# Cross rows of the ridge solves kept with the head innermost, and the complements' sides stored together

## The reference

```python
G = Kc.T @ Kc + RIDGE_EPS * I
W = jnp.linalg.solve(G, Kc.T @ Vc)
U = U0
for _ in range(POWER_K):
    U, _ = jnp.linalg.qr(W @ U)
Wr = U @ (U.T @ W)
S_new = DECAY_ALPHA * S + Wr
out = SCALE * (Qc @ S_new)
...
x = x + _L0_attn_ref(_layernorm(x, axis=-1), ...)
x = x + _L0_ffn_ref(_layernorm(x, axis=-1), ...)
```

## Time and profile before

| | |
|---|---|
| median of 3 runs | 900.69 us (897.38 to 904.1) |
| profiled execution, its own time | 900.93 us |
| its span in the profile | 899.1 us |
| mean granted TensorE clock | 0.958 |
| busy: TensorE, VectorE, ScalarE, GpSimd | 783.1, 631.7, 490.1, 227.4 us |
| TensorE weight loads, beside the matmuls | 530.6 us |
| DMA engines' mean busy share of queue 1 (SyncE's) and queue 0 (GpSimd's) | 36.8% and 7.5% |
| chain that ended last, by engine | TensorE 66%, VectorE 13%, issue 9%, DMA 5%, ScalarE 4% |

### The profile page before, as it was taken

The page is one execution under the profiler, slowest core; times in us unless marked ns, Lnnn a source line. Parts: engine busy times, 40 slices in busy tenths (PEclk is TensorE's granted clock), DMA queues, the critical chain, the costliest instruction groups (busy, mean ns, idle before and its releaser), DMA issues.

```text
span 899.1 us, 34359 instructions
## 1 busy us (share of the span) xinstructions
PE 783.1 (87%) x14730; PEld 530.6 (59%) x14730; DVE 631.7 (70%) x1336; ACT 490.1 (55%) x1068; POOL 227.4 (25%) x297
## 2 busy tenths in 40 slices
PE   4999999999999998988687687888798888899996
PEld 2555555565555555656455565666576666677775
DVE  3666399089998999980798988889953304666664
ACT  1864444555455454554444465556566665466665
POOL 4666100201001100000201012652012203555554
PEclk9999999999999999999879888999999999899999
DMA  8555211653455636655734645344456432222210
GB/s 313 155 159 167 77 62 42 205 177 122 139 162 160 185 72 168 185 162 168 162 79 119 188 116 159 103 135 116 107 154 138 104 93 69 62 82 74 77 43 30
DMA packets 174662, 114.43 MB, mean 127 GB/s; under 512 B 134128, under 2 KB 152944, under 8 KB 173488
## 3 DMA queue, kind: packets, MB, share of 16 engines
q1 hardware_dynamic: 168784, 91.00, 36.8%
q0 software_dynamic: 5728, 21.24, 7.5%
HBM read 61.22 MB, written 50.99 MB: 125 GB/s over the span
## 4 chain that ended last, share of the span: by engine, by line
PE 66%; DVE 13%; issue 9%; DMA 5%; ACT 4%; SPq 1%; POOL 1%; POOLq 0%; DVEq 0%; ACTq 0%
PE psum L1286 25%; PE psum L1332 6%; PE psum L1531 6%; PE psum L1541 5%; DVE outer L1142 4%; PE psum L1473 3%; PE psum L1511 3%; DVE work L1148 3%; PE psum L1504 2%; PE psum L1388 2%; PE psum L1375 2%; PE psum L1362 2%; PE psum L1423 2%; DVE state L1204 2%; PE psum L1497 1%
## 5 line engine op out<-in xcount | busy, mean ns | idle before, releaser
L1286 PE MATMUL psum<-wkv,xhat 128*128 128x512 f32 x512 | 240.3, 613 | 4.3 <-ACT xhat L834 4.3
L1142 DVE SCALAR_TENSOR_TENSOR outer<-work,rd 128x992 f32<-128x992 f32 (+30 forms) x248 | 189.6, 764 | 8.9 <-DVE rd L1136 0.3
L1148 DVE TENSOR_TENSOR work<-work,outer 128x992 f32<-128x992 f32 (+30 forms) x248 | 176.3, 711 | 8.6
L1286 PEld LDWEIGHTS psum<-wkv,xhat 128*128 128x128 f32 x512 | 93.2, 192 | 105.3 <-issue 99.5
L871 ACT COPY kv<-psum 128x512 f32<-128x512 f32 x128 | 75.1, 587 | 120.8 <-PE psum L1286 120.5
L1002 ACT ACTIVATE late<-psum,b1c,alpha 128x128 f32<-128x128 f32 x256 | 96.7, 461 | 49.6 <-PE psum L1531 49.6
L759 POOL TENSOR_TENSOR hsplit<-late,hsplit 128x512 f16<-128x512 f32 x64 | 77.4, 1211 | 142.4 <-ACT hsplit L1007 142.3
L1531 PEld LDWEIGHTS psum<-y3t,s1t 128*128 128x128 f16 x1024 | 61.3, 102 | 17.7 <-issue 16.7
L1531 PE MATMUL psum<-y3t,s1t 128*128 128x128 f16 x1024 | 66.9, 227 | 4.4 <-DVE y3t L1232 4.0
L1541 PE MATMUL psum<-s2t,hsplit 128*128 128x256 f16 x512 | 63.7, 279 | 4.0 <-POOL hsplit L759 2.7
L1332 PE MATMUL psum<-kv 128*64 128x128 f32 x1024 | 64.4, 280 | 0.0
(11 more groups left out here) (130 smaller groups left out, 1279.5 us busy)
## 6 DMA issues: line engine op xcount, KB each, us to landing
gc_d<-gc SPq DMA_DIRECT2D x32, 384.0 KB, 2.5
schur_mem<-gc_d SPq DMA_DIRECT2D x32, 384.0 KB, 4.2
f_d<-late SPq DMA_DIRECT2D x16, 512.0 KB, 3.6
late<-f_d SPq DMA_DIRECT2D x32, 256.0 KB, 2.7
sv_d<-sv SPq DMA_DIRECT2D x16, 384.0 KB, 3.1
lead_d<-work POOLq DMA_DIRECT2D x4, 1024.0 KB, 5.0
schur_mem<-lead_d SPq DMA_DIRECT2D x32, 128.0 KB, 4.3
r_d<-pt SPq DMA_DIRECT2D x16, 256.0 KB, 2.2
```

The lines of the kernel that those rows point to most:

```text
L1142: V.scalar_tensor_tensor(out=tile, in0=a[:, t, t + 1:HALF].unsqueeze(2).broadcast_to([P, m, HALF]), scalar=rd[:, t:t + 1], in1=a[:, t, t + ...
L1148: V.tensor_tensor(rest, rest, tile, ALU.subtract).then_inc(swept, 1)
L1286: ins = mm(dst[:], xnt[:, c, t], wkv[:, n, t, BANK * half:BANK * (half + 1)], start=t == 0, stop=t == KT - 1)
```

## The change

`pt`, `r_d` and `rr` are stored with the 32 columns outer and the 8 pairs of heads innermost. Per partition the load of `rr` is then one piece of 1 KB (32 x 8 numbers). The matmuls of SP and SX write PSUM, and those of SX and W read `pt` and `rr`, with a step of 8 numbers (32 bytes) from one column to the next. ScalarE's write of `lt`, whose layout stays, now steps by 128 bytes. `sv` and `sv_d` hold the 128 numbers of all complements first, then the 256 of all sides, so `vv` is loaded in pieces of 1 KB; ScalarE fills `sv` with two copies (128 x 256 and 128 x 512) in place of one. The unit matrices in `rr` are placed by four instructions in place of two. In the planner, MB of batch 2 or 3 is not put on the list before NB 7 or NB 15.

```diff
-                if t <= now["pe"]:
+                if t <= now["pe"] and (b < 2 or ("NB", CPB * (b - 1) - 1) in where):
                     del mask_at[b]
                     order.append(("MB", b))
...
-    r_d = scratch("r_d", [NCH, P, PAIRS, HALF])
-    sv_d = scratch("sv_d", [NCH, P, PAIRS // 2, 3 * HALF])
+    r_d = scratch("r_d", [NCH, P, HALF, PAIRS])
+
+    sv_d = scratch("sv_d", [NCH, P, PAIRS // 2 * 3 * HALF])
...
-        pt = sb("pt", [P, 2, 2, PAIRS, HALF])
+        pt = sb("pt", [P, 2, 2, HALF, PAIRS])
...
-        sv = sb("sv", [P, 2, PAIRS // 2, 3 * HALF])
+        sv = sb("sv", [P, 2, PAIRS // 2 * 3 * HALF])
...
-        rr = sb("rr", [P, 2, PAIRS, HD])
+
+        rr = sb("rr", [P, 2, HD, PAIRS])
...
-                    sp.dma_start(vv[:, i], sv_d[c + i][:, :, HALF:]).then_inc(solve_loaded, 16)
+                    sp.dma_start(vv[:, i], sv_d[c + i][:, P:].rearrange("p (s n) -> p s n", n=HD)).then_inc(solve_loaded, 16)
...
-                    sp.dma_start(rr[:, i, :, 0:HALF], r_d[c + i]).then_inc(sides_loaded, 16)
+                    sp.dma_start(rr[:, i, 0:HALF], r_d[c + i]).then_inc(sides_loaded, 16)
...
-                        src = sv_d[CPB * b:CPB * (b + 1), :, s, 0:HALF].rearrange("c (q i) n -> (c q) i n", q=QUADS)
+                        src = sv_d[CPB * b:CPB * (b + 1), :, HALF * s:HALF * (s + 1)].rearrange("c (q i) n -> (c q) i n", q=QUADS)
...
-                    nc.scalar.copy(rr[sl, :, :, HALF:].rearrange("p a h n -> p (a h) n"), eye).then_inc(eyes_placed, 1)
+                    for i in range(2):
+                        nc.scalar.copy(rr[sl, i, HALF:], ident[sl, sl].unsqueeze(2).broadcast_to([HALF, HALF, PAIRS])
+                                       ).then_inc(eyes_placed, 1)
...
-                    nc.scalar.mul(lt[rows(2 * a)].rearrange("p c h n -> p (c h n)"), src[rows(2 * a)], -1.0)
+                    nc.scalar.mul(lt[rows(2 * a)].rearrange("p c h n -> p c n h"),
+                                  src[rows(2 * a)].rearrange("p (c n h) -> p c n h", c=2, h=PAIRS), -1.0)
...
-                nc.scalar.copy(sv[:].rearrange("p c s n -> p c (s n)"), pieces(place("SV", e), BANK)[:, :, 0:12 * HALF]
-                               ).then_inc(drain("SV", e), 1)
+                src = pieces(place("SV", e), BANK)[:, :, 0:12 * HALF].rearrange("p c (s n) -> p c s n", n=3 * HALF)
+                nc.scalar.copy(sv[:, :, 0:P].rearrange("p c (s n) -> p c s n", n=HALF), src[:, :, :, 0:HALF])
+                nc.scalar.copy(sv[:, :, P:].rearrange("p c (s n) -> p c s n", n=HD), src[:, :, :, HALF:]).then_inc(drain("SV", e), 1)
...
-                dst = begin("SP", e)
+                dst = begin("SP", e).rearrange("p (c n h) -> p c n h", c=2, h=PAIRS)
...
-                            ins = mm(dst[sl, at:at + HALF], lp[sl, c, h, HALF:], lp[sl, c, h, 0:HALF], start=True, stop=True)
+                            ins = mm(dst[sl, c, :, h], lp[sl, c, h, HALF:], lp[sl, c, h, 0:HALF], start=True, stop=True)
...
-                                p, b = pt[sl, e % 2, c, h], gct[sl, e % 2, c, h, 0:HALF]
-                                ins = mm(dst[rows(2 * a + turned), at:at + HALF], b if turned else p, p if turned else b,
+                                p, b = pt[sl, e % 2, c, :, h], gct[sl, e % 2, c, h, 0:HALF]
+                                ins = mm(dst[rows(2 * a + turned), c, :, h], b if turned else p, p if turned else b,
...
-                                r, u = rr[side(a), c % 2, 2 * q + n], cu[side(a), n, c % 2, q]
+                                r, u = rr[side(a), c % 2, :, 2 * q + n], cu[side(a), n, c % 2, q]
```

More of the change, by code:

```diff
@@ L374, in build @@
         w2n = schur_mem[:, FT * DM:FT * DM + KT * FF].rearrange("p (t h) -> p t h", h=FF)
-        pt = sb("pt", [P, 2, 2, PAIRS, HALF])
-        xg = pt[:].rearrange("p e c h n -> p (e c h n)").rearrange("p (a k d) -> p a k d", a=2, k=2)
+        pt = sb("pt", [P, 2, 2, HALF, PAIRS])
+        xg = pt[:].rearrange("p e c n h -> p (e c n h)").rearrange("p (a k d) -> p a k d", a=2, k=2)
         lt = sb("lt", [P, 2, PAIRS, HALF])
-        sv = sb("sv", [P, 2, PAIRS // 2, 3 * HALF])
+        sv = sb("sv", [P, 2, PAIRS // 2 * 3 * HALF])
         lps = sb("lps", [P, 2, PAIRS // 2, HD])
         vv = sb("vv", [P, 2, PAIRS // 2, HD])
-        rr = sb("rr", [P, 2, PAIRS, HD])
+        rr = sb("rr", [P, 2, HD, PAIRS])
         cu = sb("cu", [P, 2, 2, PAIRS // 2, HD])
@@ L562, in load_solve @@
                 if e == 0:
-                    sp.wait_ge(eyes_placed, 4)
+                    sp.wait_ge(eyes_placed, 6)
                 if e % HALF_BATCH == 0:
@@ L618, in _ @@
                     sp.wait_ge(*is_drained("SX", c))
-                    sp.dma_start(r_d[2 * c:2 * c + 2].rearrange("c p h n -> p c h n"), pt[:, c % 2]
+                    sp.dma_start(r_d[2 * c:2 * c + 2].rearrange("c p n h -> p c n h"), pt[:, c % 2]
                                  ).then_inc(r_stored[c % 2], 16)
@@ L622, in _ @@
                     sp.wait_ge(*is_drained("SV", c))
-                    sp.dma_start(sv_d[2 * c:2 * c + 2].rearrange("c p s n -> p c s n"), sv[:]).then_inc(sv_stored, 16)
+                    sp.dma_start(sv_d[2 * c:2 * c + 2].rearrange("c p n -> p c n"), sv[:]).then_inc(sv_stored, 16)
                 elif step == "LS":
@@ L894, in leading_inverse @@
                 wait(act, r_stored[e % 2], 16 * (e // 2))
-                nc.scalar.copy(pt[:, e % 2].rearrange("p c h n -> p (c h n)"), place("SP", e)).then_inc(drain("SP", e), 1)
+                nc.scalar.copy(pt[:, e % 2].rearrange("p c n h -> p (c n h)"), place("SP", e)).then_inc(drain("SP", e), 1)
             def crosses(e):
@@ L902, in crosses @@
                 for a in range(2):
-                    nc.scalar.mul(lt[rows(2 * a)].rearrange("p c h n -> p (c h n)"), src[rows(2 * a)], -1.0)
+                    nc.scalar.mul(lt[rows(2 * a)].rearrange("p c h n -> p c n h"),
+                                  src[rows(2 * a)].rearrange("p (c n h) -> p c n h", c=2, h=PAIRS), -1.0)
                 for a in range(2):
-                    ins = nc.scalar.mul(pt[rows(2 * a + 1), e % 2].rearrange("p c h n -> p (c h n)"), src[rows(2 * a + 1)], -1.0)
+                    ins = nc.scalar.mul(pt[rows(2 * a + 1), e % 2].rearrange("p c n h -> p (c n h)"), src[rows(2 * a + 1)], -1.0)
                 ins.then_inc(drain("SX", e), 1)
@@ L1358, in leading_inverse @@
                     for h in range(PAIRS):
-                        at = HALF * (PAIRS * c + h)
                         for a in range(2):
                             sl = rows(2 * a)
-                            ins = mm(dst[sl, at:at + HALF], lp[sl, c, h, HALF:], lp[sl, c, h, 0:HALF], start=True, stop=True)
+                            ins = mm(dst[sl, c, :, h], lp[sl, c, h, HALF:], lp[sl, c, h, 0:HALF], start=True, stop=True)
                 ins.then_inc(fill("SP", e), 1)
             def crosses(e):
-                dst = begin("SX", e)
+                dst = begin("SX", e).rearrange("p (c n h) -> p c n h", c=2, h=PAIRS)
                 pe.wait_ge(*is_drained("SP", e))
@@ L1380, in complements @@
                 if e == 0:
-                    pe.wait_ge(eyes_placed, 4)
+                    pe.wait_ge(eyes_placed, 6)
                 dst = begin("SV", e)
```

## The result

The changed kernel takes 914.39 us (median of 4 runs, 912.71 to 919.84), the kernel before 899.04 (4 runs, 893.63 to 904.1): 1.018 of before, 95% interval 1.011 to 1.026. It is slower, by 1.1 to 2.6%. The profiled execution took 914.26 us, its span is 912.3.

What follows compares the result with a forecast made beforehand. TensorE was taken to bound 300 to 420 and 670 to 757 us, VectorE mostly 425 to 661. Costs of 9.4 us against gains of 7.0 gave +2.4 on 900.9, so 903.3 us, range 888 to 923.

Steps and rivals of the forecast that it cites:

- my likeliest case: Whole kernel: stepped operands cost part of a slowdown, offset by gains from fewer pieces; 896 to 911 us, chance 0.40.
- the halved pace: Rival: stepped operands halve TensorE's pace in W and SX, weight loads included; +20.1 us, 921 us, chance 0.27.
- The loss above 1%: Outcome for the whole kernel: slower than 910 us, beyond what a measurement can tell from no change; chance 0.32.
- Step of W: W reading `rr` with a step: 0.33 us more each, 14 of 32 counted, 4.6 us, ends 0 and 15.3.
- Step of SX: SX moving or loading stepped columns: 0.33 us more each, 12 of 16 counted, 4.0 us, top end 11.0.
- PSUM: Stepped PSUM writes of SP and SX: taken as 0, top end 13.6 us if SP takes twice as long.
- `lt`: ScalarE's stepped write between SX and SV: 588 ns to 0.92 us, mostly covered by a projection; 0.5 us, ends 0 and 8.
- `sv` in two copies: ScalarE's two copies for one: 0.17 us x 16, of which 0.3 us counts; 2.7 us without cover.
- The broken steps: TensorE gaps without instructions near `rr` and `cu` issues, 11.1 us: half the pieces, so -5.5 us, ends 0 and -11.1.
- The wait for `vv` at 669.54 us: Chain wait of 3.94 us after the last sweep: faster landing and issue give -1.5 us, ends 0 and -2.
- The queue of `cu`: SyncE's four issues of `cu`, 5.48 us, held up by what was already sent: expected well below 5.5 us.
- The planner's edit: Condition on MB of batch 2 or 3 after NB 7 or 15: always holds already, same list, worth 0.

Runs made afterwards that it cites:

- The kernel with 133,703 packets and no step: Kernel before with sides stored together and unit matrices kept in `pt` and `r_d`, so `rr` loads in 2-KB pieces, every operand contiguous; 902.69 us, 1.010 of before.

## Why the prediction was right or wrong

The forecast was 903.3 us with a range of 888 to 923; measured were 914.4, in the upper half, between my likeliest case (896 to 911) and the halved pace (921). The loss above 1% had a chance of 0.32. So the direction and the wide range held, and my own case did not: the halved pace is the rival whose mechanism the runs bear out, and my price for the step was less than half of the measured one.

- **Step of W.** I took 0.33 us more for each and gave the top end of twice as long. The chain shows 1.82 against 1.09, +0.73. For 14 steps that is 10.2 us, not 4.6. This is the first term that was mis-sized: I had priced TensorE's step by VectorE's 0.65 ns per number, and I had given the half that is loaded as weights no cost. Stepped weight loads went from 140 to 199 ns, and matmuls with a stepped moving operand from 224 to 288 ns in flight. SV with a stepped `lt` shows that a stepped load alone costs little beside a contiguous moving operand; how W's 0.73 us divide between its two halves no run shows.
- **Step of SX.** +0.33 taken, +0.94 measured (2.18 against 1.24), the top end. For 12 steps 11.3 us, not 4.0. The same error.
- **PSUM.** SP kept 1.13 us and 193 ns per matmul, so the 0 was right, and the end of 13.6 us was not needed.
- **`lt`.** 0.5 us taken, "a projection between these steps mostly"; 6.3 us more of waiting in SV. The projection is there, as I had it, and the timeline at 178 us shows why it doesn't cover: it and the transposes last 2.2 us, ScalarE's four instructions 3.3. Before, these took 2.4 us and were nearly covered, so almost all of the added 0.94 us shows. The duration went over my estimate, too (1058 ns, I had 0.92 us).
- **`sv` in two copies** (373 + 594 instead of 800 ns) and the units: nothing measurable, as forecast.
- **The broken steps.** I took half of 11.1 us. From 300 to 420 us all rows of "issue" fell from 8.1 to 0.5 us, from 670 to 770 from 7.0 to 5.9, 8.7 together. The sign and the order are right, by luck: the reason that I gave, half the pieces, is not borne out. The kernel with 133,703 packets and no step kept its stalls, and the one with all the packets and SX stepped lost a third of them. It looks as if part of what the step costs is taken out of time in which TensorE had nothing to issue.
- **The wait for `vv` at 669.54 us** is gone from the chain, as I had it, but nothing was gained by it: the last sweep's store starts 10.5 us later (672.50 against 661.97), and the next S starts at 685.17 us, 12.7 us after that store, where before it was 11.5.
- **The queue of `cu`**: 1.9 to 2.5 us for its four issues before 420 us where before the change it took 2.5 to 5.5, yet one of 3.6 us is left at 701.25 us, and the U step beside it is broken for 2.14 us.
- **The planner's edit**: the list is the same, worth 0.

The sum with the measured terms up to the fourth leading sweep: W 6 x 0.73 = 4.4, SX 11.3, `lt` 6.3, less 14.5 - 3.3 = 11.2 of stalls: +10.8. The chain shows 432.03 - 425.21 = +6.8. The 4 us between stay open; TensorE's clock, 0.97 in 300 to 420 us before and 1.00 after, could be 3.6 of them (an estimate, 3% of 120 us). It isn't the step that gave the clock: the kernel with the sides alone, where nothing steps, has 1.00 in that stretch as well.

That kernel is also the nearer neighbour for a sum, since the cross rows are all that parts it from the changed one. Its load starts at 413.7 us, so from there the rows cost 18.3 us. Its stalls from 165 us to the load are 8.1 us against 3.9, its SV waits 1.8 us for ScalarE against 8.0, and the terms give 4.4 + 11.3 + 6.2 - 4.2 = 17.7. So the prices of W, SX and `lt` account for this stage. The profile of the kernel before has 16.2 us of stalls in this stage, twice its neighbour's 8.1, so part of the fall in stalls that I read from it is the spread of single executions.

Of the 13.2 us between the spans of before and after, 6.8 are there at that load, 3.7 more come by the store of the last sweep, and 2.7 behind it. The eight W steps behind it would be 5.8 us alone; that part I didn't take apart.

The windows of the kernel after (stretch, PE, PEld, DVE, ACT, POOL busy with counts, clock, DMA share, GB/s), against the earlier trace rows:

```profile
300.00:420.00 120.00, 117.35 (x2520) 74.59 (x2514) 102.28 (x190) 68.20 (x132) 6.48 (x10) 1.00 0.55 161
...
670.00:760.00 90.00, 82.00 (x2272) 62.34 (x2271) 23.37 (x66) 54.53 (x134) 19.16 (x27) 1.00 0.41 117
```

TensorE is busy for 117.35 of 120 us, and still the stage ends 6.8 us later: the higher busy share here is more time for the same work.

## What to carry to other kernels

- Before an fp32 operand of TensorE is given a step for the sake of a DMA, look where two neighbouring columns lie: 8 bytes apart cost nothing here, 16 or 32 bytes apart took steps from 1.09 to 1.8 us and from 1.24 to 2.2, while a step whose weights alone were 32 bytes apart lost only 0.03. Heads in groups of two keep TensorE's pace and halve the pieces of `rr` (256 bytes instead of 128), though that gained no time here. And ScalarE did the reordering of `lt` for free (588 ns) by reading PSUM with a step and writing SBUF without one.
- Work that covers a wait covers it only up to its own length. Here 2.2 us of TensorE's work between two steps nearly hid ScalarE's 2.4 us, and didn't hide its 3.3: compare the two lengths before a longer instruction is called free.
- A stall of TensorE beside many small DMAs is not yet caused by them. Here a kernel with a quarter fewer packets had as many; the test is to take the pieces away with everything else left alone.
- No version here beats the kernel before by more than can be measured: the sides alone stand at 0.998 (0.9945 to 1.0014).

## What the runs showed of the hardware

- W and SX, whose fp32 operand steps as moving and as stationary operand, took 1.67 and 1.76 times as long with a step of 32 bytes (1.82 against 1.09 us, 2.18 against 1.24), nearly the same at 16 bytes as at 32 (stepped weight loads 195 and 199 ns against 140), and next to nothing more at 8 (143).
- SV, in which only the weights step by 32 bytes, beside 96 contiguous moving columns, took mostly 1.48 to 1.55 us against 1.45 to 1.52, though its loads went from 114 to 138 ns.
- PSUM took TensorE's fp32 columns with a step of 32 bytes at full pace (193 ns against 192), and gave them to ScalarE so (588 ns). The Trainium skill (page Advanced Engine Details and Errata, section Memory Cachelines) has any non-contiguous pattern in PSUM slow matmuls; the measurement decides against it for these.
- ScalarE's write of 512 fp32 numbers to SBUF costs 1058 ns with a step of 128 bytes, 588 without.
- TensorE's idle time without a releaser was 22.2 to 35.3 us in the seven kernels in which its operands step by 16 bytes or more, and 36.8 to 49.2 in the seven others, whatever the number of DMA packets.
- A load whose source is one piece of 1 KB kept its queue time (`vv`, 506 against 530 ns), while `rr` came down from 618 to 442 ns in the median, 320 at best.
